# A graph network on one core: gathers released by free slots alone, and normalised sums made two units ahead of the residuals

## What is computed

```python
def gatv2_layer(x, Wl, bl, Wr, br, att, bias, src, dst, n):      # H = 8 heads, C = 32 channels
    xl = (x @ Wl + bl).reshape(n, H, C)
    xr = (x @ Wr + br).reshape(n, H, C)
    e = leaky_relu(xl[src] + xr[dst], 0.2)
    logits = einsum('ehc,hc->eh', e, att)
    m = segment_max(logits, dst, num_segments=n)
    p = exp(logits - m[dst])
    alpha = p / (segment_sum(p, dst, num_segments=n)[dst] + 1e-16)
    out = segment_sum(xl[src] * alpha[:, :, None], dst, num_segments=n)
    return out.mean(axis=1) + bias
...
h = gatv2_layer(x, Wl[l], bl[l], Wr[l], br[l], att[l], conv_bias[l], src, dst, n)   # l = 0, 1, 2
x = batchnorm_train(leaky_relu(h, 0.01) + x, bn_gamma[l], bn_beta[l])              # no leaky_relu at l = 2
...
x = layernorm(x + first_network(x))
x = layernorm(x + second_network(x))
```

## Time and profile before

| | us |
|---|---|
| median of 3 runs | 7853.58 |
| lowest and highest | 7843.77, 7854.25 |
| the profiled execution | 7840.21 |
| its span, first to last instruction | 7838.1 |

### The profile page before, as it was taken

One profiled execution on the slowest core, in us unless ns is written; L12 is line 12 of the kernel. 1 busy time (PEld: TensorE's weight loads), 2 busy tenths in 40 slices (PEclk: granted clock), 3 DMA queues, 4 the chain that ended last, 5 costly groups with the idle time before them and its releaser, 6 DMA issues.

```text
span 7838.1 us, 176242 instructions
## 1 busy us (share of the span) xinstructions
PE 6163.7 (79%) x26512; PEld 4656.6 (59%) x26513; DVE 6394.4 (82%) x12894; ACT 3281.8 (42%) x11055; POOL 4875.5 (62%) x8226
## 2 busy tenths in 40 slices
PE   0688888885478888888547888888854999999998
PEld 0366666664446666655435656665544888888887
DVE  7688888885468888888547888888846999999999
ACT  0255545553125545445313545444511444444444
POOL 1888878870288878885038878887412555555554
PEclk8899999998599999999759999999965555555555
DMA  2211111110011111111001111111101111111111
GB/s 87 49 34 33 37 31 34 34 30 0 9 36 34 37 31 34 33 36 22 0 15 36 36 32 34 33 36 31 19 0 31 30 30 30 30 30 30 30 30 28
DMA packets 214500, 237.82 MB, mean 30 GB/s; under 512 B 72973, under 2 KB 195854, under 8 KB 213902
## 3 DMA queue, kind: packets, MB, share of 16 engines
q1 hardware_dynamic: 93582, 163.43, 7.2%
q0 software_dynamic: 120704, 72.40, 6.9%
HBM read 222.34 MB, written 13.20 MB: 30 GB/s over the span
## 4 chain that ended last, share of the span: by engine, by line
issue 27%; DVE 22%; PE 21%; POOL 12%; DVEq 11%; DMA 3%; POOLq 3%; ACT 1%; ACTq 0%; SPq 0%
POOL xg L506 7%; PE psum L637 6%; PE psum L622 6%; POOL idx L483 4%; DVE xs L1525 3%; PE psum L715 2%; DVEq L1510 2%; DVE acc L1537 2%; DMA xg<-table,idx 2%; DVEq L1189 2%; DVEq L990 2%; DVE u L1155 2%; PE psum L705 2%; PE psum L610 2%; PE psum L624 1%
## 5 line engine op out<-in xcount | busy, mean ns | idle before, releaser
L506 POOL DMA_INDIRECT xg<-table,idx x2808 | 2877.3, 1025 | 754.4 <-issue 278.0
L622 PE MATMUL psum<-wz,xt 128*128 x5928 | 1820.5, 401 | 51.2 <-ACT xt L890 49.7
L637 PE MATMUL psum<-px,oh 128*128 128x272 f32 x5616 | 1632.5, 414 | 161.2 <-DVE acc L1196 80.6
L819 ACT ACTIVATE dist<-iota_f,ndloc 128x128 f32<-128x128 f32 x2808 | 974.2, 394 | 1512.5 <-PE psum L637 1500.6
L637 PEld LDWEIGHTS psum<-px,oh 128*128 128x128 f32 x5616 | 961.7, 191 | 516.0 <-DVE acc L1196 210.8
L622 PEld LDWEIGHTS psum<-wz,xt 128*128 128x128 f32 x5928 | 1024.4, 197 | 384.6 <-ACT lin L837 72.5
L771 PE MATMUL psum<-w2e,xt 65*128 65x256 f32 x1872 | 1056.6, 668 | 228.7 <-DVE xs L1525 175.3
L552 POOL DMA_INDIRECT xg<-table,idx x936 | 905.4, 967 | 384.5 <-issue 242.2
L1163 DVE TENSOR_REDUCE lr<-u 128x16 f32<-128x512 f32 x1482 | 1012.8, 686 | 158.7 <-DVE u L1155 117.3
L1182 DVE TENSOR_TENSOR px<-xs,pg 128x528 f32 (+1 forms) x1404 | 997.1, 710 | 109.0 <-issue 47.7
L1155 DVE SCALAR_TENSOR_TENSOR u<-psum,atts 128x512 f32<-128x512 f32 x1482 | 1017.3, 686 | 71.0 <-PE psum L624 69.2
(11 more groups left out here) (270 smaller groups left out, 8379.7 us busy)
## 6 DMA issues: line engine op xcount, KB each, us to landing
dr<-dlocs SPq DMA_DIRECT2D x468, 192.0 KB
xg<-table,idx POOLq DMA_INDIRECT x3744
at<-w_rows SPq DMA_DIRECT2D x156, 192.0 KB
fl<-flags SPq DMA_DIRECT2D x30, 576.2 KB
flags<-fl SPq DMA_DIRECT2D x10, 576.2 KB, 3.1
table<-xn SPq DMA_DIRECT2D x3, 784.0 KB, 3.6
xp<-keys SPq DMA_DIRECT2D x5, 385.0 KB, 4.5
u<-keys SPq DMA_DIRECT2D x5, 385.0 KB, 4.4
```

Source lines behind the costliest of these rows:

```text
L506: nc.gpsimd.indirect_dma_start(out=xg[:, s % S6, t, 96:128], out_offset=None, in_=table, in_offset=bass.IndirectOffsetOnAxis(ap=idx[:, s, ...
L622: pe.matmul(out_z, xt[:, r, e * P:(e + 1) * P], wz[:, bass.ds(l, 1), :].rearrange("p o z -> p (o z)"), start=True, stop=False)
L637: last = pe.matmul(agg_ps(r), oh[:, r, e, :], px[:, r, e, :], start=(e == 0), stop=(e == 1))
L819: last = op.activation(dist[:, e, :], iota_f[:], ACT.Abs, bias=ndloc[:, bass.ds(k, 1), e])
```

## The change

Two edits. First, the gathers of the attention layers lose their two further waits: a gather now waits for its slot (front k-6), the kept rows of step k-6 and its index column. Second, at the end of a layer VectorE runs normalized(0) and normalized(1) first, and then normalized(m+2) before residual(m). TensorE, ScalarE and GpSimd keep their orders there.

```diff
                     for t in range(2):
-                        if t == 0:
-                            pool.wait_ge(oht_done, AHEAD + l * NS + k0 + s + 1 - 3)
-                        else:
-                            pool.wait_ge(r_done, AHEAD + l * ZS + k0 + s + 1 - 8)
                         pool.wait_ge(idx_done, AHEAD + l * NUMBERS + (k0 + s) * 2 + t + 1)
...
-                normalized(l, 0, 0)
+                for r in range(2):
+                    normalized(l, r, r)
                 with v.Fori(0, SELF // 2 - 1) as i:
                     for r in range(2):
-                        normalized(l, i * 2 + r + 1, 1 - r)
+                        normalized(l, i * 2 + r + 2, r)
                         residual(l, i * 2 + r, r)
-                normalized(l, SELF - 1, 1)
                 residual(l, SELF - 2, 0)
                 residual(l, SELF - 1, 1)
```

## The result

| | before | after |
|---|---|---|
| median of the runs | 7848.7 us (4 runs) | 7423.7 us (4 runs, 7420.9 to 7424.9) |
| ratio | | 0.9461, 95% interval 0.9445 to 0.9477 |
| span of the profiled execution | 7838.1 us | 7418.7 us |
| groups 1 to 8 of a layer, mean of 24 | 158.2 us | 152.0 us |
| group 9, up to the next layer part, mean of 3 | 198.2 us | 192.4 us |

From L501 on, a line's number in the changed kernel is four smaller than before: the gather is L502, the front's matmul L609, the output matmul L711, the one-hot L1146, the first weighing instruction L1151, px L1178, the residual begins at L1335.

A forecast was written before the change was run, and what follows sets the result against it. GpSimd was taken to drive part of the groups, a ring without overlap the end of a layer. 7840.2 - 251 (end of layer) - 113 (gathers) = 7476, plus 13.4 for the median: 7490 us; range 7440 to 7575.

The forecast's parts named there:

- 0.4 us of cover: End of a layer: TensorE's unit of 3.86 us against 3.44 us for VectorE, so TensorE becomes the bound.
- Rival 3: End of a layer: TensorE's clock rises to 2.4 GHz, 42 us less, 7448 us; chance 0.10, shared with larger gather gains.
- the head start: Group start: steps 3 to 5 gathered in 10.2 idle us, step 10 about 8 us earlier; gathers' gain 113 us.
- VectorE's pace is 17.3 a body: Inside a group: VectorE takes 2.88 us a step against GpSimd's 3.09, so the gathers' lead shrinks 8.0 us over 38 steps.
- the free group: A group whose gathers' lead lasts to about its end: 153.6 us against 158.5, a gain of 4.9 us.
- the 0.3 for long instructions: Maxima stage: 0.3 us a group taken off for gathers now running beside VectorE's long instructions; bounds 0 and 10.2 us.
- 48 x 3.09 = 148.3 us is the floor: Groups: GpSimd's own pace over 48 steps limits how short a group can get, 148.3 us.
- if bodies get shorter than 17.3: Groups: VectorE waits less for TensorE, and up to 8 us a group come in.
- Rival 1: Groups: the gathers give nothing, bodies of 18.6 us being TensorE's or VectorE's own; 7603 us, chance 0.15 with rival 5.
- Rival 2: End of a layer: GpSimd's xp falls into VectorE's sums or residual each time; 79 us more, 7569 us, chance 0.07.
- Rival 4: Groups: TensorE's clock falls to 1.2 GHz, a step loses 2.1 us; about 8960 us on half the steps, chance 0.01.
- The lead runs out early: Groups: the gathers' lead ends two bodies early, 2 x 1.3 us lost per group, and 113 us becomes some 50.

The follow-up runs named there:

- e11: Changed kernel with the third of the three products that add up a unit's output (L711) left out; 7415.3 us, ratio 0.9440 to the kernel before.
- e8: Changed kernel with the copy of each pair's 64 gathered columns (L491) moved from GpSimd to ScalarE; 7316.8 us, ratio 0.9308 to the kernel before.
- e4b: Changed kernel with one gather wait back, for the channel sums of eight steps earlier; 7506.2 us, ratio 0.9559 to the kernel before.
- e2b: Kernel before with only the two further waits of the gathers taken out, the end of the layer as it was; 7679.8 us, ratio 0.9780.
- e7: Changed kernel with VectorE's weighted rows (px, L1178) made with one buffer operand instead of two; 7301.2 us, ratio 0.9294 to the kernel before.

## Why the forecast was too high

*End of the layer: right in size.* Forecast 251 us, measured 251 alone; by the trace 3 x (184.1 - 98.6) = 256. The unit is 3.79 us instead of 3.86. The forecast named TensorE as the only bound with 0.4 us of cover; e11 shows that VectorE, with L1337 held by xp, stands level with it, so that there was no cover; the size came out right because a bound that was not seen lay just at the one that was. Rival 3 is out: a full array kept the granted clock of 0.50. (Its 3.3 us for VectorE has no row; the 3.44 of the text above it would have made it 32 us and not 42.)

*Gathers: the head start right, what holds the freed group wrong, 113 against about 175 us.* Steps 3 to 5 are gathered in the time that stood idle and the wait for front 0 follows, as forecast. The step that failed is "VectorE's pace is 17.3 a body": the price of the free group, 16.6 + 6 x 17.3 + 33.2 = 153.6 us, let VectorE's second body hold the group. That body is 17.2 after the change too, but it is a single one: the next are 16.95, and bodies 1 to 6 together take 102.7 us where 103.8 were counted. The last body with the maxima stage takes 32.6 where 33.2 and the 0.3 for long instructions were counted. The free group is 152.0 us and not 153.9 (and the group before 158.2 on average, where 158.5 was taken). What holds it is GpSimd, which reaches VectorE's floor of 148.9 only when its own step is cut (e8). A us of its stop is worth 0.8 us of the group: the stops went from 10.7 to 3.2 us, 7.5 less, and the group lost 6.2 where I counted 4.6; e4b gives the same rate. The missing fifth is GpSimd's own work, which grew by 1.3 us a group, among other things because 13.0 gathers a group instead of 11.6 begin inside px.

The forecast's "48 x 3.09 = 148.3 us is the floor" was the nearer side, but not right as it stood either: with the stop that its rows give for front 0 (3230.34 + 9.27 to 3240.80, 1.2 us) it makes 149.5 us, 9 us a group. The forecast did name this direction, "if bodies get shorter than 17.3", with up to 8 us a group, gave it a share of the 0.10 of rival 3, and left its far end out of the range. In groups 1 to 8 the step missed 1.6 us x 24 = 38 us.

*The last groups: 3 us forecast, 17 measured.* Group 9 has the same stop at its start and the same GpSimd, and it gains nearly the same (198.2 to 192.4). I gave it 1 us each with no row behind it. This is 14 us of the miss.

*Two small ones.* The gather beside the maxima stage's long instruction takes 1.75 us where it took 1.58 before, so the 0.3 us a group for that price was enough. Group 0 lost 0.7 us each, where I had said that it gains nothing.

*By the trace:* 38 + 14 from the groups, 6 from the end of the layer and 2 lost in group 0 make 56 of the 55 us by which the spans' difference (419) passes the forecast's 364.

*Rivals.* Rival 1 (the gathers give nothing) is out by e2b. Rival 2's lock exists but was covered. Rival 4 did not come: the granted clock over the groups of layer 1 is 0.95, as before (single stretches show 0.93 to 0.99). "The lead runs out early" is true of some groups: bodies 5 and 6 are 17.2 and 17.5 us on average.

## What to carry to other kernels

Ask first which engine holds a whole period, and do not answer from the pace of one piece of it, such as a second body. An engine's own work and its stops add up to the period whether it holds it or not (147.5 + 10.7 us in the kernel before, where GpSimd held it, 136.3 + 12.6 in e8, where it did not). What tells them apart is whether the engine, once released, runs to the end of the period without another stop while the others fall into its pace, as the late bodies of 18.5 us did before, and an experiment that shortens its work alone. Where it does hold the period, a us off its stops was worth 0.8 us here, down to the next engine's floor. An idle time has no price in itself: 274 us of it cost 175 in one kernel, and 308 us cost 17 in another, where the waiting engine had slack. And a fully busy engine can have another right behind it, at the same pace, so shorten both before counting on either.

## What the runs showed of the hardware

- A gather that begins inside VectorE's px, a product of two operands in the buffer, takes 1.32 us on average in the changed kernel (334 gathers, up to 1.51), and 0.98 when it begins inside L1151, L1159 or L1192, which have one operand in the buffer (1675 gathers). With a one-operand px (e7) those that begin inside it take 1.07. The Trainium skill (SBUF — State Buffer, "Who interferes with whom") says that tensor_tensor does not hold up the writing of descriptors; the length of these gathers doesn't agree. A gather also reads its index column from the buffer, and no run here separates the two.
- VectorE's L1337, two operands in the buffer, takes 0.28 us alone. When it begins inside GpSimd's xp of 1.05 us it ends 0.08 us after xp does, so that it takes 0.29 to 0.34 us late in xp (the changed kernel) and mostly 0.61 to 0.73 early in it (e11).
- TensorE at work for 97.00 of 97 us, on transposes of 99 columns and matmuls of 32, was granted 0.50 (1.2 GHz) throughout, as it was when half idle in the same stage before. The Trainium skill (TensorE: Matmul & The Clock Gate, "What's actually happening") would have a busy engine go to 2.4 GHz; this stretch does not follow it.
- Of four chips that ran the kernel before beside the experiments, three took 7855 to 7856 us and one 8584. On the slow one the instructions took as long as on the others, but ScalarE and VectorE paused for some 28 and 22 us more a group with no releaser in the core; the granted clock in like stretches was 0.85 against 0.95, and the worth of one wait was 214 us instead of 77.
